# The layers' edge stage: each block's four lists loaded in halves, one list per step, and five blocks of turned rows

## What is computed

```python
for i in range(L):
    Q = _ln(h @ Wq[i], gq[i], bq[i])
    K = _ln(h @ Wk[i], gk[i], bk[i])
    qi = Q[src]
    kj = K[dst]
    score = (qi * kj).sum(-1) + 0.1 * (edge_attr * qi[:, :RBF]).sum(-1) + logm[dst]
    smax = jax.ops.segment_max(score, src, num_segments=N)
    es = jnp.exp(jnp.minimum(score - smax[src], 20.0))
    denom = jax.ops.segment_sum(es, src, num_segments=N)
    alpha = es / (denom[src] + 1e-10)
    m = h[dst] @ Wm[i]
    aggi = jax.ops.segment_sum(alpha[:, None] * m, src, num_segments=N)
    z = jnp.concatenate([h, aggi], axis=-1) @ Wu[i]
    z = jnp.where(z > 0, z, 0.01 * z)
    h = _ln(h + z, go[i], bo[i])
```

## Time and profile before

| | us |
|---|---|
| three runs of the kernel before | 5669.24, 5683.79, 5712.89 |
| their median | 5683.79 |
| profiled execution, its own time | 5691.99 |
| span of its instructions | 5690.3 |
| granted clock of PE, mean of the span | 0.81 |
| edge stages of the four layers (SP's first load to the last sum) | 1963.5 to 2415.0, 2512.8 to 2961.8, 3059.0 to 3514.4, 3611.5 to 4065.7 |
| busy in these four stages together (1810.1 us) | PE 1567.0, ACT 1466.7, DVE 1403.2, POOL 1229.3 |
| mean share of the DMA engines' time that was busy in them | 0.41 to 0.42 |

### The profile page before, as it was taken

How to read it: one execution, slowest core, us unless ns; L and a number is a source line. 1 busy time by engine, 2 the same in 40 slices (tenths; PEclk the granted TensorE clock), 3 DMA queues, 4 the chain that set the end, 5 groups by cost and what they waited for, 6 DMA issues and landing times. The chain is left out here.

```text
span 5690.3 us, 187291 instructions
## 1 busy us (share of the span) xinstructions
PE 4165.3 (73%) x78576; PEld 3539.3 (62%) x78576; DVE 3801.8 (67%) x8933; ACT 2695.5 (47%) x8154; POOL 2674.8 (47%) x2702
## 2 busy tenths in 40 slices
PE   6999994036666498858976987689567844978886
PEld 3555552025555388748865886588546733977786
DVE  6888875069999588668856876688585446435244
ACT  3333331036666388748865886588502424100410
POOL 2777777756666277617752764377321510000000
PEclk7666665569999699869987997899787977988897
DMA  9322222257677444344424442544165443000000
GB/s 353 79 73 73 71 69 66 53 122 204 192 198 192 118 164 156 112 101 174 159 90 130 164 156 74 147 166 158 52 111 210 145 125 101 3 9 4 4 4 10
DMA packets 480771, 652.91 MB, mean 115 GB/s; under 512 B 315712, under 2 KB 362948, under 8 KB 476693
## 3 DMA queue, kind: packets, MB, share of 16 engines
q1 hardware_dynamic: 443541, 591.08, 33.7%
q0 software_dynamic: 33856, 48.44, 3.5%
q10 hardware_dynamic: 2496, 0.98, 0.1%
HBM read 460.24 MB, written 180.09 MB: 113 GB/s over the span
## 5 line engine op out<-in xcount | busy, mean ns | idle before, releaser
L299 POOL DMA_INDIRECT edges<-sb_bk_rec,sb_bk_pos x782 | 782.6, 1001 | 325.2 <-issue 234.4
L1728 ACT ACTIVATE sb_at_val<-banks,sb_at_prob 128x49 f32<-128x49 f32 x3800 | 785.9, 356 | 73.3 <-PE banks L1653 66.7
L1776 DVE CUSTOM_DVE_ANT_0 sb_at_left<-banks,sb_at_others 128x512 f32<-128x512 f32 x1000 | 646.0, 661 | 231.1 <-PE banks L1634 221.8
L1613 PE MATMUL banks<-sb_near,sb_at_hotT_d 128*128 128x49 bf16 x11100 | 621.6, 185 | 71.2 <-issue 51.2
L1615 PE MATMUL banks<-sb_queryp,sb_at_hotT_s 128*128 128x49 bf16 x11400 | 637.2, 186 | 38.6 <-issue 38.6
L1613 PEld LDWEIGHTS banks<-sb_near,sb_at_hotT_d 128*128 128x128 fp8e4 x11100 | 566.8, 97 | 76.2 <-issue 69.9
L1615 PEld LDWEIGHTS banks<-sb_queryp,sb_at_hotT_s 128*128 128x128 fp8e4 x11400 | 566.3, 97 | 44.3 <-issue 43.9
L1573 POOL TENSOR_TENSOR sb_at_key<-sb_at_key,sb_at_attr 128x400 f32<-128x400 f32 (+1 forms) x400 | 373.9, 935 | 460.2 <-ACT sb_at_key L1701 448.8
L1711 ACT ACTIVATE sb_at_others<-sb_at_hotT_s,sb_at_minus_big 128x1536 bf16<-128x1536 fp8e4 (+2 forms) x400 | 535.8, 1340 | 3.9 <-DVE sb_at_tops L1776 3.9
L1653 PE MATMUL banks<-sb_near,sb_at_hotT_d 128*128 128x49 bf16 x11100 | 368.6, 187 | 70.3 <-issue 37.7
L1580 POOL TENSOR_TENSOR sb_at_val<-sb_at_val 128x490 f32<-128x490 f32 (+1 forms) x400 | 387.1, 968 | 67.3 <-ACT sb_at_val L1728 65.9
(11 more groups left out here) (696 smaller groups left out, 10299.9 us busy)
## 6 DMA issues: line engine op xcount, KB each, us to landing
sb_at_attr<-attr SPq DMA_DIRECT2D x100, 760.0 KB, 7.6
sb_at_hotT_s<-rows_src_t SPq DMA_DIRECT2D x100, 608.0 KB, 5.5
sb_at_hot_s<-rows_src SPq DMA_DIRECT2D x100, 608.0 KB, 8.7
sb_at_hotT_d<-rows_dst_t SPq DMA_DIRECT2D x100, 592.0 KB, 6.9
edges<-sb_pad SPq DMA_DIRECT2D x95, 460.0 KB
sb_gt_rec<-edges SPq DMA_DIRECT2D x25, 1748.0 KB
sb_we_hotT<-rows_dst_t SPq DMA_DIRECT2D x52, 592.0 KB, 5.9
attr<-sb_gt_rec SPq DMA_DIRECT2D x25, 760.0 KB, 12.9
```

The source lines that it names most:

```text
L299: pool.indirect_dma_start(list1, bass.IndirectOffsetOnAxis(pos[:, t:t + 1], 0), rec[:, k, j, :], None).then_inc(sent[k], 16)
L1613: pe.matmul(ps[:, 0, H1 * j:H1 * j + H1], where, what, start=(n == 0), stop=(n == 2))
L1728: ins = act.mul(val[:, v % VB, j, 0, :], ps[:, 5, H1 * j:H1 * j + H1], prob[:, i % 2, k:k + 1])
L1776: dve.tensor_tensor_reduce(left[:, x % 2, 0:n], ps[:, 3 + x % 2, 0:n], others[:, w % 2, ks[0] - first:ks[-1] + 1 - first, :].rearrange("p ...
```

## The change

SP's program of the stage is written anew. Every list is sent in two halves: tiles 0 to 19, and tiles 20 to 37 (to 36 for `hotT_d`). Each step of the stage sends one list of one block: step 4i sends `hotT_s` of block i + 1, step 4i + 1 its `hotT_d`, step 4i + 2 its `attr`, and step 4i + 3 sends `hot_s` of block i - 2. Ahead of the first half SP waits for the end of that step's `keys` (`s_keys`), ahead of the second for the end of that step's `total` (`s_sum`; in the early steps, which have no `total`, for `s_score`). The turned rows get five places in place of four (`HT` = 5), and the waits of PE and POOL count two halves. The same bytes are loaded, and no work of PE, ACT, DVE or POOL is added, removed or moved.

```diff
+HT = 5
...
-            def first(i):
-                if i >= 4:
...
-                    sp.wait_ge(s_h, Q * (i - 3))
-                sp.dma_start(flat(hotT_s, i % 4), lists["hotT_s"][i]).then_inc(s_hotT[i % 4], 16)
-                sp.dma_start(flat(hotT_d, i % 4), lists["hotT_d"][i]).then_inc(s_hotT[i % 4], 16)
...
-            attributes(0)
-            for i in range(1, NB + 3):
-                if i < NB:
-                    first(i)
-                    attributes(i)
-                if i >= 3:
-                    last(i - 3)
+            def half(to, src, w, h):
+                a, b = ((0, 20), (20, KT))[h]
+                b = min(b, to.shape[1])
+                return to[:, a:b, :].rearrange("p k e -> p (k e)"), src[:, w * a:w * b]
+
+            def sources(i, h):
+                if h == 0 and i >= HT:
+                    sp.wait_ge(s_h, Q * (i - HT + 1))
+                sp.dma_start(*half(hotT_s[:, i % HT], lists["hotT_s"][i], P, h)).then_inc(s_hotT[i % HT], 16)
...
+            def attributes(i, h):
+                if h == 0 and i >= 2:
                     sp.wait_ge(s_key, Q * (i - 1))
+                sp.dma_start(*half(attr[:, i % 2], lists["attr"][i], RBF, h)).then_inc(s_attr[i % 2], 16)
+
+            def last(i, h):
+                if h == 0 and i >= 2:
                     sp.wait_ge(s_sum, Q * (i - 1))
+                sp.dma_start(*half(hot_s[:, i % 2], lists["hot_s"][i], P, h)).then_inc(s_hots[i % 2], 16)
+
+            def in_step(u, h):
+
+                v = u - LAG - 3 + h
+                if h == 0 and u < U:
+                    sp.wait_ge(s_keys, u + 1)
+                elif v > 0:
+                    sp.wait_ge(s_sum, v)
+                elif u:
+                    sp.wait_ge(s_score, u)
+            for h in range(2):
+                attributes(0, h)
+            for u in range(Q * (NB + 2)):
+                i, q = divmod(u, Q)
+                load, n = ((sources, i + 1), (targets, i + 1), (attributes, i + 1), (last, i - 2))[q]
+                if 0 <= n < NB:
+                    for h in range(2):
+                        in_step(u, h)
+                        load(n, h)
...
-                    pool.wait_ge(s_attr[i % 2], 16 * (i // 2 + 1))
+                    pool.wait_ge(s_attr[i % 2], 32 * (i // 2 + 1))
...
-                    pe.wait_ge(s_hotT[i % 4], 32 * ((i - 1) // 4 + 1 if i % 4 else i // 4))
+                    pe.wait_ge(s_hotT[i % HT], 64 * (i // HT + (1 if i % HT else 0)))
```

More of the change, by code:

```diff
@@ L1522, in attend @@
              "h", "val", "rest", "split2", "sum", "added", "link", "minus", "others"]
-    rings = [f"attr{k}" for k in range(2)] + [f"hots{k}" for k in range(2)] + [f"hotT{k}" for k in range(4)] + [
+    rings = [f"attr{k}" for k in range(2)] + [f"hots{k}" for k in range(2)] + [f"hotT{k}" for k in range(HT)] + [
         f"far{k}" for k in range(4)]
@@ L1528, in attend @@
             s_prob, s_h, s_val, s_rest, s_split2, s_sum, s_added, s_link, s_minus, s_others, *dmas):
-        s_attr, s_hots, s_hotT, s_far = dmas[0:2], dmas[2:4], dmas[4:8], dmas[8:12]
+        s_attr, s_hots, s_hotT, s_far = dmas[0:2], dmas[2:4], dmas[4:4 + HT], dmas[4 + HT:8 + HT]
         @block.sync
@@ L1533, in _ @@
             flat = lambda v, k: v[:, k].rearrange("p k e -> p (k e)")
-            def first(i):
-                if i >= 4:
-                    sp.wait_ge(s_h, Q * (i - 3))
-                sp.dma_start(flat(hotT_s, i % 4), lists["hotT_s"][i]).then_inc(s_hotT[i % 4], 16)
-                sp.dma_start(flat(hotT_d, i % 4), lists["hotT_d"][i]).then_inc(s_hotT[i % 4], 16)
-            def attributes(i):
-                if i >= 2:
+            def half(to, src, w, h):
+                a, b = ((0, 20), (20, KT))[h]
+                b = min(b, to.shape[1])
+                return to[:, a:b, :].rearrange("p k e -> p (k e)"), src[:, w * a:w * b]
@@ new lines, in sources, with targets @@
+            def sources(i, h):
+                if h == 0 and i >= HT:
+                    sp.wait_ge(s_h, Q * (i - HT + 1))
+                sp.dma_start(*half(hotT_s[:, i % HT], lists["hotT_s"][i], P, h)).then_inc(s_hotT[i % HT], 16)
+            def targets(i, h):
+                if h == 0 and i >= HT:
+                    sp.wait_ge(s_h, Q * (i - HT + 1))
+                sp.dma_start(*half(hotT_d[:, i % HT], lists["hotT_d"][i], P, h)).then_inc(s_hotT[i % HT], 16)
+            def attributes(i, h):
+                if h == 0 and i >= 2:
@@ L1544, in attributes @@
                     sp.wait_ge(s_key, Q * (i - 1))
-                sp.dma_start(flat(attr, i % 2), lists["attr"][i]).then_inc(s_attr[i % 2], 16)
-            def last(i):
-                if i >= 2:
+                sp.dma_start(*half(attr[:, i % 2], lists["attr"][i], RBF, h)).then_inc(s_attr[i % 2], 16)
+            def last(i, h):
+                if h == 0 and i >= 2:
                     sp.wait_ge(s_sum, Q * (i - 1))
-                sp.dma_start(flat(hot_s, i % 2), lists["hot_s"][i]).then_inc(s_hots[i % 2], 16)
@@ L1596, in place @@
                 if k < NW:
-                    return hotT_d[:, i % 4, k, :], near[:, k, n, lo:lo + H1]
+                    return hotT_d[:, i % HT, k, :], near[:, k, n, lo:lo + H1]
                 return c["identb"][:], far[:, i % 4, n, lo:lo + H1]
@@ L1614, in keys @@
                     for n in range(3):
-                        ins = pe.matmul(ps[:, 1 + u % 2, H1 * j:H1 * j + H1], hotT_s[:, i % 4, k, :], queryp[:, i, n, :],
+                        ins = pe.matmul(ps[:, 1 + u % 2, H1 * j:H1 * j + H1], hotT_s[:, i % HT, k, :], queryp[:, i, n, :],
                                         start=(n == 0), stop=(n == 2))
@@ L1642, in maxima @@
                 for k in range(KT):
-                    ins = pe.matmul(ps[:, 7, 3 * k:3 * k + 3], hotT_s[:, i % 4, k, :], high(mparts[:, i % 2, :]), start=True, stop=True)
+                    ins = pe.matmul(ps[:, 7, 3 * k:3 * k + 3], hotT_s[:, i % HT, k, :], high(mparts[:, i % 2, :]), start=True, stop=True)
                 ins.then_inc(s_mgot, 1)
@@ L1659, in total @@
                 if q == 0:
-                    pe.wait_ge(s_hots[i % 2], 16 * (i // 2 + 1))
+                    pe.wait_ge(s_hots[i % 2], 32 * (i // 2 + 1))
                     if i:
@@ L1710, in apart @@
                     act.wait_ge(s_rowk, Q * i + 1)
-                act.activation(others[:, n % 2, 0:b - a, :], hotT_s[:, i % 4, a:b, :], ACT.Identity, bias=minus_big[:], scale=BIG
+                act.activation(others[:, n % 2, 0:b - a, :], hotT_s[:, i % HT, a:b, :], ACT.Identity, bias=minus_big[:], scale=BIG
                                ).then_inc(s_others, 1)
@@ L2573, in first_part @@
             near = t.sb("near", [P, NW, 3, KH], BF16)
-            hotT_s, hotT_d = t.sb("at_hotT_s", [P, 4, KT, P], F8), t.sb("at_hotT_d", [P, 4, NW, P], F8)
+            hotT_s, hotT_d = t.sb("at_hotT_s", [P, HT, KT, P], F8), t.sb("at_hotT_d", [P, HT, NW, P], F8)
             first = [(hotT_s[:, 0].rearrange("p k e -> p (k e)"), lists["hotT_s"][0]),
```

## The result

The changed kernel takes 5590.8 us (median of four runs, 5568.1 to 5594.4). The kernel before, on the same chip, takes 5688.5 (5669.2 to 5712.9). The ratio is 0.9832, with a 95% interval of 0.9811 to 0.9853: about 98 us gained, where 172 were forecast. The time lies 79 us above the predicted 5512. It is inside the range over all cases (5465 to 5615) and 21 us above 5570, where the range of the forecast case itself ended.

A forecast was written before the change was run, and what follows sets the result against it. PE and ACT were both near nine tenths busy, PE stalling for instruction refills behind list bursts. Blocks falling from 16.93 to 14.95 us (14.65 plus 0.3), times 87, save 172 us: 5512 us, range over all 5465 to 5615.

The forecast's parts named there:

- forecast case: Whole kernel: spreading the lists ends most of PE's stands; 5512 us, own range 5465 to 5570, chance 0.72.
- "nothing" case: Rival: PE's stands come from its own stream, or total traffic holds the refill; 5684 us, chance 0.08.
- "slower" case: Rival: a refill's loss goes by bytes sent, not burst length; 108 us slower, 5792 us, chance 0.07.
- undisturbed block: Steps 12 to 99: four undisturbed steps of the earlier trace sum to 14.45 to 14.82 us; 14.65 taken per block.
- engines making up for time lost before: Sign of being wrong: steps stay at 4.2 us without stands, so the 3.4 to 3.8 us steps were catching up.
- What was left of the stands: Steady part: refills still delayed behind single pieces cost 0.3 us a block, 26 us over 87 blocks.
- bound from `gather_sums`: Another stage's 1.2 MB pieces lose 1.37 us each, implying 0.4 us reserve; here 0.4 us a block.
- reserve of 1 to 2 us: Refill delay PE bears before it stands, against about 1 us of data per piece; leftover loss then 0.
- The ends: Steps 0 to 11 and the drain behind step 99: no change, 0 with 10 us either way.
- The added waits and issues: SP issues 8 times a block in place of 4; each half lands in time by 1.5 us or more; cost 0.
- "half of it" case: Rival: queueing holds refills longer than each piece's data, leaving 0.8 us of stands a block; 5596 us, chance 0.13.
- The signs: If right: "issue" under 35 us, windows about 325, clock 0.99 or 1.00, PE share about 0.97, no late list.

The follow-up runs named there:

- e4: The changed kernel with each list from block 5 on cut to its first tile, leaving out most loads; 5565.5 us.
- e1: The kernel before with five places for the turned rows and nothing else; 5693.9 us, ratio 0.9990.
- e2: The changed kernel with a block's eight halves sent together in one burst behind one wait; 5666.6 us, ratio 0.9933.
- e3: The changed kernel with whole lists in place of halves, one per step behind that step's keys; 5592.1 us, ratio 0.9806.
- e9: The changed kernel with DVE's four small operations as reductions over an axis of length one, leaving out mask, split and shift's sum; 5522.1 us.
- e10: The changed kernel with the four small DVE operations as reductions and lists from block 5 on cut to their first tile; 5473.5 us.
- e8: The changed kernel with lists from block 5 on cut to their first tile and four small DVE operations in one-input forms with a constant; 5548.3 us.
- e7: The changed kernel with lists in thirds, waiting for the end of the step's keys, values and total in turn; 5568.0 us, ratio 0.9826.

## Why the prediction came out as it did

**The mechanism was right.** PE stood because its refills came late while a burst drained. The prediction inferred that from one stand; the counts over all bursts and all 104 stands bear it out. What on the DMA engines a refill stands behind is open. Three refills arrive among the pieces now, the stands fall from 146.9 to 37.1 us, and with the lists cut short (e4) 3.6 us of them are left in the steady part. e1 and e2 leave the burst and keep the stands; e3 takes only the burst away, and they go from 144.5 to 43.1 us. The "nothing" case (stands of PE's own stream, or of the total traffic) and the "slower" case (loss by the byte) are excluded by e3: the same bytes, a third of the loss. The rule of the Trainium skill that spoke against the change ("Runtime: NRT & Kernel Launch", section "Instruction fetch mechanics": the refill is mostly hidden) does not describe these rows: the stands came and went with the burst.

**The step that failed is the one that set the undisturbed block to 14.65 us.** Undisturbed the block is 15.32 us by its medians, 0.67 more than assumed, and 58 us over 87 blocks. The prediction took four steps of the earlier trace rows from different blocks of a stage in which every block had a burst. About 0.17 of the 0.67 lies in the rows themselves: for the second step it took the middle between 3.83 and 4.20, but 3.83 is what 25 of the 81 undisturbed steps of this kind take, and their median is 4.20, which gives 14.82.

The other 0.5 is the wait for DVE, 0.19 us in the first step and 0.3 in the second. In the kernel before the split took 0.91 us a block on average, and PE never waited for `at_sparts` in the steady part. Without stands it takes 1.54 (1.75 in e4) and PE waits. The table of runs shows it in the main: the fewer the stands, the longer the first and third operation (the reductions aside). Why DVE meets POOL less often behind a stand is argued and not shown: PE's stand is time in which DVE works off what it owes. That the wait costs this much is shown: with the four operations short the undisturbed block takes 14.57 us. The prediction named "engines making up for time lost before" as a sign itself, for steps that stay at 4.2 us; the last two steps, 3.49 and 3.40, came out as it had them, and only the first two did not. It also took steps in which "ACT runs without idle time" as proof that ACT was the floor. ACT was busy for 14.6 of 15.3 us in the undisturbed block, and PE for 14.8, so that 14.65 was near what both need, but not what the block takes while PE waits for DVE. Its remark that "the data by itself slows neither engine" holds: e9 and e10 differ by 0.04 us in the undisturbed block. That DVE's small operations have two lengths stood in the kernel before too, and I hadn't looked at them.

**What was left of the stands** was set to 0.3 us a block, 26 us in all. It is 0.44 us of stands (37.9 / 87), and with the clock 0.51 (15.83 - 15.32), 18 us more than assumed over 87 blocks. One such place in the timeline of PE, and the window behind it, whose clock reads 0.63 (part of it at 1.2 GHz, part at 2.4):

```profile
3750.07 0.63 PE L1674 MATMUL banks<-sb_near,sb_at_hotT_d 128*128 128x49 bf16 x18 [1.21 <-issue]
```

```profile
3750.10:3754.70 4.60, 4.60 (x96) 4.60 (x97) 2.64 (x6) 1.86 (x10) 0.87 (x1) 0.63 0.26 66
```

The estimate by the bound from `gather_sums` (0.4) was nearer than the reserve of 1 to 2 us, which gave 0. But its picture, a loss that goes by the length of a piece, doesn't fit e3: by the same formula its four pieces of about 2 us would lose 1.4 us a block (an estimate), and 0.5 us was measured (43.1 / 87).

**The ends** were set to 0 with 10 us either way. The first twelve steps of the four layers take 163.9 us for 156.8; the drain is unchanged (42.8 us a layer). Part of it is the first block's attributes, which land in two halves. POOL's wait for them, first before, then after:

```profile
POOL sb_at_key L1573 <- DMA sb_at_attr<-attr: 11.4, 4, 2.9
```

```profile
POOL sb_at_key L1594 <- DMA sb_at_attr<-attr: 15.0, 4, 3.9
```

**The added waits and issues** cost nothing, as said: these four waits of POOL are the only ones for a list.

Together: 58 + 18 + 7 = 83 us less gain than forecast. From 5512 that is 5595, and 5591 was measured. That this is so close is in part luck: the forecast counted from 5684 us, and the kernel before takes 5688.5 by four runs; and in the two profiles the parts ahead of the four stages and behind them, which the change doesn't touch, are 19 us shorter, while the stretches between the layers are 5 us longer. The time came out within 5 us of the "half of it" case (5596), and by another mechanism than that case names: the pieces do not give back half in stands, the block has a second limit that the stands had covered.

Three of the prediction's figures are off and change nothing. The four lists are 2568 KB, which is 2.63 and not 2.57 MB. The first two windows of the earlier trace rows are 731 us together, not 733. And the forecast's own upper bound of 5570 doesn't follow from 0.7 us left a block: 14.65 + 0.7 gives 5546, 14.95 + 0.7 gives 5572.

**The signs**, as the prediction listed them: "issue" under 35 us, measured 37.1; clock 0.99 to 1.00, right; no late list, right; windows of about 325 us, measured 342 to 346, wrong; PE's busy share 0.97, measured 0.95, wrong. "Issue" missed by 2 us. The last two come for the larger part from DVE's small operations: with them short (e9) the windows are 329 to 332 us and the share is 0.97.

## What to carry to other kernels

Spread large loads over the time in which they are needed: one list a step did it, and cutting it up further brought nothing that the kernel's time shows by itself. An undisturbed time cannot be put together from pieces of a disturbed run, since a stall of one engine lets the others catch up and shifts where they meet; look for what the others would hold up once it is gone, above all for groups of equal instructions with unequal durations. Small VectorE operations beside a busy GpSimd cost what GpSimd's running operation has left, as two-input operations and those with a constant did here, unless they are of a form that doesn't wait, as the reduction was.

## What the runs showed of the hardware

- A VectorE operation of 128 x 38 fp32 takes 0.20 us (two tiles as input) or 0.18 (one and a constant) alone. If it begins while a GpSimd TENSOR_TENSOR of 1 us runs, it ends 0.04 to 0.07 us after that one and takes up to 1.05 us (161 of 162 in the changed kernel, all 186 in e8). As a reduction it takes 0.19 in all 400 cases.
- While 2568 KB that were sent at once drain, hardly a packet of the instruction queue starts (8 in the three microseconds from 1 to 4 us behind the first issue, over 84 bursts, for 16 to 28 in each microsecond ahead of it), and PE stands for up to 3.5 us, until 1.2 to 1.6 us after the end of the next packet. With single pieces of 592 to 760 KB, one a step, 43.1 us of stands are left of 144.5 (e3), with pieces of some 190 to 260 KB 10.1 (e7), with few bytes 3.6 (e4).
- Behind a stand of 1.21 us the granted clock was 0.63 for 4.6 us; behind the stand of 2.93 us in the earlier trace rows it was 0.50 for 6.8 us.
